# Item rows turned into columns by copying DMAs and one matmul each, a load on two queues, three memsets placed later, in a graph kernel

## The reference

```python
def _graph_conv(x, src, dst, out_norm, in_norm, W, b):
    h = x * out_norm[:, None]
    agg = jax.ops.segment_sum(h[src], dst, num_segments=N_NODES)
    return (agg * in_norm[:, None]) @ W + b
# block 0: norms from the degrees of src and dst; three _graph_conv, each followed by elu
x = _layernorm(x + block0(x))
# block 1: one convolution with edge attributes, then an MLP with batch norm
ea = edge_attr @ W_edge.T + b_edge
agg = jax.ops.segment_sum(jax.nn.relu(x[src] + ea), dst, num_segments=x.shape[0])
h = (x + agg) @ W1.T + b1
h = relu(gamma * (h - mean) * rsqrt(var + BN_EPS) + beta)
x = _layernorm(x + h @ W2.T + b2)
```

## Time and profile before

| | value |
|---|---|
| median of three runs | 5930.7 us |
| the profiled execution's own time | 5929.95 us |
| its span | 5927.5 us |
| PE busy | 5126.1 us, 86% |
| DVE busy | 4312.7 us, 73% |
| POOL busy | 3753.5 us, 63% |
| ACT busy | 2273.7 us, 38% |
| instructions | 112,214 |

### The profile page before, as it was taken

How to read it: one execution, slowest core, us unless ns; L and a number is a source line. 1 busy time by engine, 2 the same in 40 slices (tenths; PEclk the granted TensorE clock), 3 DMA queues, 4 the chain that set the end, 5 groups by cost and what they waited for, 6 DMA issues and landing times.

```text
span 5927.5 us, 112214 instructions
## 1 busy us (share of the span) xinstructions
PE 5126.1 (86%) x39907; PEld 3126.5 (53%) x39908; DVE 4312.7 (73%) x14548; ACT 2273.7 (38%) x4057; POOL 3753.5 (63%) x3824
## 2 busy tenths in 40 slices
PE   7999799999879999999999994777877877777776
PEld 6566566667654555555555442444444444444445
DVE  5899888889995555656666323888888877777776
ACT  2888689887630000000001111343434433333333
POOL 4523223336625777777777777777777777777773
PEclk9999899999999999999999997999999988888886
DMA  2622334433217878788989982221222222222221
GB/s 89 262 114 115 129 141 146 145 143 120 92 68 253 288 276 272 274 277 273 272 271 281 300 287 69 44 44 43 45 43 43 44 41 41 41 41 41 41 41 38
DMA packets 438341, 828.25 MB, mean 140 GB/s; under 512 B 161611, under 2 KB 266983, under 8 KB 430951
## 3 DMA queue, kind: packets, MB, share of 16 engines
q1 hardware_dynamic: 305430, 713.88, 35.5%
q0 software_dynamic: 117952, 81.54, 7.0%
q10 hardware_dynamic: 14400, 25.61, 1.5%
HBM read 621.34 MB, written 199.35 MB: 138 GB/s over the span
## 4 chain that ended last, share of the span: by engine, by line
PE 39%; POOL 34%; issue 13%; DVE 7%; ACT 5%; DMA 1%; POOLq 0%; DVEq 0%; ACTq 0%; SPq 0%
POOL rows_f L1108 28%; PE banks L2204 21%; PE banks L2126 6%; POOL sorted_recs L1073 6%; PE banks L2091 5%; ACT wide L1889 4%; DVE rows_f L1369 3%; DVE rows_f L1364 3%; PE banks L2098 2%; PE banks L2179 1%; PE banks L2186 1%; PE banks L2152 1%; PE banks L2036 1%; DMA agg_a<-attr_dram 1%; PE banks L2047 0%
## 5 line engine op out<-in xcount | busy, mean ns | idle before, releaser
L1108 POOL DMA_INDIRECT rows_f<-table,src_key x1725 | 1654.5, 959 | 525.7 <-issue 525.7
L1073 POOL DMA_INDIRECT sorted_recs<-onehot,rows x1280 | 1237.2, 967 | 493.6 <-issue 394.7
L1889 ACT ACTIVATE wide<-banks 128x784 fp8e4<-128x784 f32 x1563 | 1204.7, 825 | 324.4 <-PE banks L2126 322.7
L1028 POOL DMA_INDIRECT onehot<-edge_runs_dram,rows_f x472 | 626.2, 1327 | 949.2 <-DVE onehot L1218 739.1
L2204 PE MATMUL banks<-wide,rows_f 128*128 128x512 fp8e4 (+1 forms) x4900 | 1128.0, 376 | 16.0 <-issue 12.1
L2126 PE MATMUL banks<-rows_f 128*128 128x196 f16 (+2 forms) x7525 | 1002.3, 257 | 103.7 <-DVE rows_f L1369 55.8
L2126 PEld LDWEIGHTS banks<-rows_f 128*128 128x128 f16 x7525 | 708.8, 152 | 480.8 <-ACT wide L1889 305.3
L2293 PE MATMUL banks<-w_edge_blk,rows 80*128 80x320 f32 x690 | 299.3, 519 | 565.8 <-DVE rows_f L1674 485.6
L2091 PE MATMUL banks<-wide,onehot 128*128 128x392 fp8e4 x3125 | 782.7, 331 | 0.3 <-ACT wide L1889 0.3
L1364 DVE TENSOR_TENSOR rows_f<-hid 128x1024 f16<-128x1024 f16 (+1 forms) x1016 | 679.4, 669 | 136.3 <-PE banks L2126 130.3
L1369 DVE TENSOR_TENSOR rows_f<-rows_f,tmp 128x1568 f16<-128x1568 f16 (+1 forms) x874 | 714.8, 818 | 0.0
(11 more groups left out here) (345 smaller groups left out, 7380.2 us busy)
## 6 DMA issues: line engine op xcount, KB each, us to landing
wide<-counts SPq DMA_DIRECT2D x504, 896.0 KB
counts<-wide SPq DMA_DIRECT2D x50, 3136.0 KB
rows_f<-table,src_key POOLq DMA_INDIRECT x1725
sorted_recs<-onehot,rows POOLq DMA_INDIRECT x1280
sorted_recs<-rows SPq DMA_DIRECT2D x28, 640.0 KB
rows<-attr_dram SPq DMA_DIRECT2D x345, 40.0 KB
onehot<-edge_recs_dram SPq DMA_DIRECT2D x143, 90.0 KB
agg_a<-attr_dram ACTq DMA_DIRECT2D x50, 250.0 KB
```

The lines of the kernel that those rows point to most:

```text
L1028: G.indirect_dma_start(out=stage[:, c % STAGES, j, :], out_offset=None, in_=edge_runs[:, :], in_offset=bass.IndirectOffsetOnAxis(ap=run_id ...
L1073: G.indirect_dma_start(out=sorted_recs[:, :], out_offset=bass.IndirectOffsetOnAxis(ap=keys_of(t, t + 1).bitcast(I32), axis=0), in_=taken[g ...
L1108: G.indirect_dma_start(out=g_rows[:, n % ROW_RING, k, :], out_offset=None, in_=table32[:, :], in_offset=bass.IndirectOffsetOnAxis(ap=src_k ...
L1889: A.activation(win_counts[o.half % 2][:, :, d0:d0 + o.quads * QUAD].rearrange("p b (q c) -> p b q c", c=QUAD), counted, ACT.Copy, scale=UN ...
```

## The change

- The loads of `fold` are split. SP loads partitions 0 to 61, ACT partitions 62 to 124. Both add to `s_fold`, and its waiters (SP, VectorE, and the counts of the fills that use the semaphore afterwards) wait for 32 instead of 16.
- ACT waits for POOL's d0 row and issues two DMAs that copy one partition of chunks 2 to 58 into a square, `d0_square`, with one chunk on each of 57 partitions; then it waits for the k row and does the same into `k_square`. Two DMAs each, because each row lies in two tensors. The squares lie in the unused end of `wide`.
- TensorE turns each square with one matmul against the identity (57 columns), instead of 57 matmuls for each row.
- VectorE's memsets of both `win_words`, of `stat` and of `rows16_f` move from before the wait for `fold` to behind `find_runs(1)`.
- VectorE's find_tile(5) moves behind ident16 and unpack(0); TensorE's turn(0) moves ahead of its wait for ident16.

```diff
+FOLD_SPLIT = 62
+        d0_square, k_square = (in_row[0:CHUNKS - 2, n * P:(n + 1) * P] for n in range(2))
+        s_square = [sem(f"s_square{n}") for n in range(2)]
-        s_fill, FILL0 = s_fold, 16
+        s_fill, FILL0 = s_fold, 32
+        fold_rows = dst_rows.rearrange("(f t) e -> f (t e)", f=FOLD)
         def _(sp):
-            sp.dma_start(fold, dst_rows.rearrange("(f t) e -> f (t e)", f=FOLD)).then_inc(s_fold, 16)
-            sp.wait_ge(s_fold, 16)
+            sp.dma_start(fold[0:FOLD_SPLIT, :], fold_rows[0:FOLD_SPLIT, :]).then_inc(s_fold, 16)
+            sp.wait_ge(s_fold, 32)
...
             V.memset(steps[0:1, FC:FC + 1], 0.0)
-            for h in (1, 0):
-                V.memset(win_words[h], 0).then_inc(s_zero, 1)
-            V.memset(stat[:, 3, :], 0.0)
-            V.memset(rows16_f.bitcast(I32), -2 ** 31).then_inc(s_zero, 1)
 
             fold3 = fold.rearrange("p (t e) -> p t e", e=P)
-            dve.wait_ge(s_fold, 16)
+            dve.wait_ge(s_fold, 32)
...
             find_runs(0)
             find_runs(1)
+            for h in (1, 0):
+                V.memset(win_words[h], 0).then_inc(s_zero, 1)
+            V.memset(stat[:, 3, :], 0.0)
+            V.memset(rows16_f.bitcast(I32), -2 ** 31).then_inc(s_zero, 1)
             dve.wait_ge(s_k, 2)
             link(V.tensor_copy(k_col[:, 2:CHUNKS], k_ps[1][:, 2:CHUNKS]))
-            for n in range(2, len(SETS)):
+            for n in range(2, len(SETS) - 1):
                 find_tile(n)
             dve.wait_ge(s_rows_k, 2)
             dve.wait_ge(s_tri, 4)
             V.tensor_copy(ident16[:, :], ident[:, :]).then_inc(s_ident, 1)
             unpack(0)
+            find_tile(len(SETS) - 1)
...
+            def square(cells, into, split, signal):
+
+                act.dma_start(into[0:split - 2, :], cells(2 * P, split * P)[0:1, :].rearrange("o (c e) -> o c e", e=P)).then_inc(signal, 16)
+                act.dma_start(into[split - 2:CHUNKS - 2, :], cells(split * P, SLOTS)[0:1, :].rearrange("o (c e) -> o c e", e=P)).then_inc(signal, 16)
+
+            act.dma_start(fold[FOLD_SPLIT:FOLD, :], fold_rows[FOLD_SPLIT:FOLD, :]).then_inc(s_fold, 16)
+            act.wait_ge(s_rows_d0, 2)
+            square(d0_cells, d0_square, D0_SPLIT // P, s_square[0])
+            act.wait_ge(s_rows_k, 1)
+            square(k_cells, k_square, K_SPLIT // P, s_square[1])
             columns(0)
...
             search(0)
             search(1)
-            pe.wait_ge(s_rows_d0, 2)
-            columns_of(d0_cells, d0_ps[1], 2, CHUNKS, s_d0)
-            pe.wait_ge(s_rows_k, 1)
-            columns_of(k_cells, k_ps[1], 2, CHUNKS, s_k)
+            pe.wait_ge(s_square[0], 32)
+            M(d0_ps[1][:, 2:CHUNKS], d0_square, ident[0:CHUNKS - 2, 0:CHUNKS - 2], start=True, stop=True).then_inc(s_d0, 1)
+            pe.wait_ge(s_square[1], 32)
+            M(k_ps[1][:, 2:CHUNKS], k_square, ident[0:CHUNKS - 2, 0:CHUNKS - 2], start=True, stop=True).then_inc(s_k, 1)
             for n in range(2, len(SETS)):
                 search(n)
+            turn(0)
             pe.wait_ge(s_ident, 2)
-            turn(0)
```

## The result

The changed kernel has a median of 5897.94 us in six runs (5895.52 to 5903.58) beside 5930.42 us for the kernel before in the same rounds (5929.60 to 5934.74): a ratio of 0.9945, with a 95% interval of 0.9935 to 0.9955. It is faster by 32.5 us, clear of the 0.2%, and lies 4 us above the range of 5879 to 5894. The profiled execution took 5903.58 us (span 5901.7), the slowest of the six.

A forecast was written before the change was run, and what follows sets the result against it. The setup chain before the item loop was taken as the bound, chiefly TensorE's 48.73 us of column matmuls. Terms from the load's 21.4 sum to a loop start of 69.4, not 111.90: 42.5 us less, 5888.2 us, range 5879 to 5894.

The forecast's parts named there:

- The load: Destination rows on two queues: both halves begin at the same two engines, 38 rows each at 0.478 us, landing at 21.4.
- The memsets: VectorE's 14.5 us moved behind find_runs(1): the first reduction waits for the load alone, but search(4) waits, costing 6.9 us.
- The columns: TensorE's 228 column instructions (48.73 us) give way to four copying DMAs and two matmuls, leaving nothing on the path.
- the 5.9 us taken from the gathers: Upper bound taken for a copy out of one partition, from the median landing of a gather of 128 rows.
- The cover of 13 us: Margin before TensorE would wait for the d0 copy: gone if d0 took 13 us more.
- Rival B: Copies into the squares go number by number, making the kernel slower, 6667 us on one engine; chance 0.03.
- VectorE's and TensorE's order: Setup sequence on both engines from the first reduction at 21.4 to the item loop at 69.4.
- POOL's 30 us to spare: POOL's gathers in setup: near_rows(2) ends near 79, its user find_runs(2) comes at 111, so POOL doesn't limit.
- 0 to 1 us at find_runs(0): VectorE's possible wait for gathered rows landing by 37.2 but wanted at 36.2; taken as 0.
- rival A: The split load lands no later, at 15.2, making the chain 6.2 us shorter and the time 5882; chance 0.25.
- Everything behind moves with the loop's start: From the item loop on, all work shifts with its start, since POOL waits there 670.6 us for VectorE's unpacking.
- The sum: Setup terms up to the item loop add to 69.4 in place of 111.90, 42.5 us less.

The follow-up runs named there:

- e1: Changed kernel with the destination rows loaded whole by one DMA on SP's queue again; median 5894.2 us, ratio 0.9936 to the kernel before.
- e4: Changed kernel with the load split into 86 rows on SP and 39 on ACT; median 5901.8 us, ratio 0.9951 to the kernel before.
- e10: Changed kernel with the load split into 34 rows on SP and 91 on ACT; 5886.0 us in one run.
- e3: Changed kernel, load still split 62 and 63, with the memsets back in front of the wait for the load; median 5891.1 us, ratio 0.9930.
- e7: Changed kernel with the load split into 60 rows on SP and 65 on ACT; median 5889.1 us, ratio 0.9927 to the kernel before.
- e9: Changed kernel split at 60, POOL's k row written behind its first two gathers, memsets in other places; median 5886.0 us, ratio 0.9923.
- e6: Changed kernel with columns made by one matmul a chunk again, without squares or their copying DMAs; median 5929.7 us, ratio 0.9997 to the kernel before.
- e5: The kernel before, unchanged, measured and profiled once more; median 5927.6 us, ratio 0.9998.
- e8: Changed kernel split at 60, memsets spread over three places where VectorE would wait; median 5877.5 us, ratio 0.9912 to the kernel before.
- e2: Changed kernel with one whole load and the memsets back in front of its wait; median 5892.6 us, ratio 0.9932 to the kernel before.

## Why the prediction was right and where it failed

*The load* (21.4): this step failed. The number of engines and the meeting of both queues on the same two were right (share 0.57 up to 6 us, 0.12 up to 10). The price was mis-sized: 38 rows at 0.478 us was taken from a load with five engines, and on these two a row took up to 0.77 us once SP's half ran alone. It came 7.0 us later than forecast, 28.4, so the split cost 13.5 us against e1 instead of 6.2. e4 and e10 put that on the split, 31 rows an engine: by the skill's map on the distance of 31 between the two engines' rows, which is argued and not shown. Of the 9.7 us between the 5888.2 forecast and the 5897.9 measured, these 7.0 are the greater part.

*The memsets*: right in size and place. The wait of search(4) was put at 6.9 us and is 6.78; e3 without it starts the loop 7.0 us earlier. With the load as late as it really was, the memsets would have been hidden where they were.

*The columns*: right. In the changed kernel TensorE doesn't wait for the copies: the k copies, issued at 24.97 and 25.79 in e7, were there at 28.0, 2.2 us after the start of the last issue; the 5.9 us taken from the gathers was too high, and had no effect. With an earlier load the wait appears (1.96 us in e1, 7.49 in e7), but ends before the ranks do; in e9 it is on the path. The cover of 13 us was misread: from the forecast landing of d0 at 22 to TensorE's asking at 30.3 it is 8.3. e6 shows that without the squares nothing is gained. Rival B fell with this.

*VectorE's and TensorE's order* up to the loop: 48.2 us from the first reduction against 48.0.

*POOL's 30 us to spare*: right for the loop (near_rows(2) ends at 86.9, find_runs(2) starts at 117.7). But the mutual hold of POOL and VectorE, for which the prediction had only 0 to 1 us at find_runs(0), accounts for the 3.8 us by which e1 missed rival A's 63.2 (67.0): 2.2 in the first rank and 1.6 in TensorE's wait, 8.49 where 6.9 was forecast. In the changed kernel it fell beside the path (POOL's second gather took 3.70 us, and find_runs(1) didn't wait).

*Everything behind moves with the loop's start*: right to 3 us. The first scattered record comes at 1788.7 instead of 1821.3 us, 32.6 earlier, after 35.3 at the loop's start. In e5 this stretch repeats that of before to 0.2 us; in e1, e3, e7, e8 and e9 it loses 2.5 to 3.2 us, in e4 0.6, and in e2, e6 and e10 it wins 0.6 to 4.8. ACT's waits for its attribute loads are not the cause: between 700 and 1,300 us those for agg_b are 2.9 us in the changed kernel against 1.1 before, but they are 2.9 in e2 too, which wins 2.0. What it depends on stays open. So does part of what follows: in each of the eight kernels with squares and several runs the median gains less than the loop's start, by 0.2 us (e3) to 6.6 (e4), which with so few runs can be spread, or not.

*The sum*: 42.5 forecast, less 7.0 of the load and 2.7 in the loop, is 32.8; the medians differ by 32.5. That the two agree to 0.3 us is partly luck, as the interval of the ratio is 12 us wide. The profiled execution shows less (its span is 25.8 us shorter), as its gather stretch was 3.9 us longer than in the low profile of before, and its records 3.2; e5 shows that as spread. The range was too narrow by 4 us because the load's upper bound was missing: rows taken from a load with other partners were used as if an engine's speed were its own.

## What to carry to other kernels

Many small matmuls that only turn a row are well replaced by a copying DMA into a square and one matmul, if the source is ready early: here 36 us for four DMAs and four instructions. Test each part of a change alone: this one would have been 10.2 us better at the loop without two of its parts. Before a load is split, look at the number of rows in each part: 125 rows went over five engines, 62 over two, 60 and 65 over fifteen and thirteen, and the load's end moved from 15 us to 28 or to below 10.6. And work moved off the path in front of one wait must be put into another engine's slack, not just later: the same memsets held TensorE up for 6.78 us behind find_runs(1) (12.02 with the early load of e7) and for 0.23 us when spread over three waits, at the price of searches that start 2.9 us later.

## What was not expected of the hardware

Two DMA engines, busy throughout (a share of 0.12 to 0.13 of sixteen), moved 33 to 37 GB/s with 31 rows each and 51 to 52 with 43 rows each. VectorE's rank of 125x6144 took 6.53 us beside POOL's iotas and 3.41 to 3.50 alone, and POOL's issue of a gather 3.70 to 3.90 us beside the rank and 0.94 to 1.10 alone. One and the same kernel's stretch of 1,725 gathers took 2179.0 us in one execution and 2186.1 in another.
